# Routing tables of a two-stage expert kernel: one compare-and-scale instruction for each tile and choice on VectorE, in place of wide compares and a scaling pass on ScalarE

## The chip, the cores and the metric

The kernel runs on one core of a Trainium2 chip. The metric is the device time of one launch in microseconds (us). Of the kernel before there are three timed runs and one profiled execution. Numbers are float32; fp32r is the rounded form of it that the products of TensorE read.

## The reference, cut to what matters

4096 rows (8 sequences of 512) of 256 numbers pass four layers: an attention layer, a mixture of 8 experts with 2 chosen for each row, a recurrent mixing layer, and the same mixture of experts again. What matters here is what comes before each expert layer: the rows have to be sorted by expert.

```
scores = softmax(x @ gate_w.T);  top_scores, sel = top_k(scores, 2)
order = argsort(sel_flat, stable)       # rows grouped by expert
tok_sorted = order % N                  # which token stands at which sorted place
```

## The kernel before

The 4096 tokens are 32 tiles of 128 (one token for each partition), and each has two choices. The kernel has four phases: attention, experts, mix, experts. Attention and mix both end with the building of a table `row_token`: for each block of 128 sorted rows, the token of every row. The expert phase gathers its rows by that table, so it starts only when the table is there (all engines meet between two phases).

**How the table is made.** `posf` holds the sorted position of each token and choice; `positions` (L287) turns it to an integer and splits it into a lane (low 7 bits, `lane_at`) and a block (the rest, `block_at`). The tiles are taken in 8 groups of 4 (`CH` is 4). For group n:

- `hot_blocks` (L302), VectorE: a 0/1 table `block_hot`, 128 x (2 choices x 4 tiles x 120 blocks), that is 1 where the block number is the token's. One compare of 960 columns, line L308, with an integer operand that is spread along the columns and `lane`, a constant ramp.
- `hot_rows` (L313), VectorE: the same for the lane, 2 x 4 x 128 = 1024 columns, one compare, line L318, output fp32r.
- `send_tokens` (L322), ScalarE: four copies with a scale for each partition, L330, 240 columns each, that multiply `block_hot` by the token's number and write `sent` in fp32r.
- `place_tokens` (L395), TensorE: 8 products (choice x tile), L401, `sent` against `row_hot`, added up in one bank over all 8 groups.

After group 7, `region_rows` (ScalarE, L337) copies the bank, `final_places` (VectorE, L363, last instruction L377) makes `spot`, `order_tokens` (TensorE, L411) multiplies the two, and `row_tokens` (VectorE, L382 and L383) writes the table.

**Buffers.** `block_hot` is 2 deep in attention and 3 deep in mix; `sent` and `row_hot` are 3 deep in attention and 6 deep in mix. `hot_blocks` waits until ScalarE has used its buffer, `hot_rows` and `send_tokens` until TensorE has.

**The order around it, written out by hand.** The groups 0 to 5 ("early") cover tiles 0 to 23, whose choices are known one sequence before the end. In attention VectorE does, after its last period: `positions`, blocks(0), the statistics of the last sequence (L827, L830), rows(0), then blocks and rows of groups 1 to 5, then the top two experts of the last sequence (`softmax_begin`, first instruction MAX8 at L135), the late choices, `late_places` (which calls `positions` again), blocks and rows of groups 6 and 7, `final_places`, `row_tokens`. ScalarE puts its `send_tokens` between the steps of the last sequence's normalisation and gate. TensorE places group 0, then the gate transposes (L991), group 1, the gate products (L1002), groups 2 to 4, the count of the late choices, groups 5 to 7.

In mix, groups 0 to 3 stand inside VectorE's last period, ahead of `finish(b, 0)` (L1944), which joins the second half of a layer for GpSimd to add to x (L1786). Groups 4 and 5 follow, then the softmax of the sequence before the last (MAX8, L135), `finish(b, 1)`, the statistics of the last sequence, its softmax, and the late part as in attention. GpSimd turns the statistics into scales in four short instructions (L772 to L775 in attention, L1754 to L1759 in mix). An instruction that the next one reads is followed by a wait for it (`own.link`).

The three instructions of the step, shortened:

```
nc.vector.tensor_tensor(r.block_hot[n % depth], block_at..to_broadcast(shape), lane[:, 0:RB]..to_broadcast(shape), ALU.is_equal)
nc.vector.tensor_tensor(r.row_hot[n % depth], lane_at..to_broadcast(shape), lane..to_broadcast(shape), ALU.is_equal)
nc.scalar.activation(r.sent[..][:, :, j, :], r.block_hot[..][:, :, j, :], ACT.Copy, scale=const.token[:, t:t + 1])
```

Of the kernel before, what the change touches and what calls it, by code (L numbers as in the profile page):

```python
# [9 lines left out]
ALU = mybir.AluOpType  # L10
ACT = mybir.ActivationFunctionType
# [200 lines left out]
class Route:  # L212


    def __init__(self, hots, ranks, small, rounded, row_hot, block_hot, sent, bank, placed, sem):
# [9 lines left out]
        self.lane_at, self.block_at = s.take([P, TOPK, T], I32), s.take([P, TOPK, T], I32)  # L225
        self.counti = s.take([P, EX], I32)
# [4 lines left out]
        self.block_hot = [Shelf(f).take([P, TOPK, CH, RB]) for f in block_hot]  # L231
# [9 lines left out]
        self.block_hot_ready, self.row_hot_ready = sem("r_block_hot_ready"), sem("r_row_hot_ready")  # L241
        self.sent_ready, self.sent_used = sem("r_sent_ready"), sem("r_sent_used")
        self.region_ready, self.spot_ready, self.table_done = sem("r_region_ready"), sem("r_spot_ready"), sem("r_table_done")
# [57 lines left out]

def hot_blocks(nc, dve, r, const, n):  # L302

    depth = len(r.block_hot)
    if n >= depth:
        dve.wait_ge(r.sent_ready, n - depth + 1)
    shape = [P, TOPK, CH, RB]
    nc.vector.tensor_tensor(r.block_hot[n % depth], r.block_at[:, :, n * CH:(n + 1) * CH].unsqueeze(3).to_broadcast(shape),  # L308
                            const.lane[:, 0:RB].unsqueeze(1).unsqueeze(1).to_broadcast(shape),
                            ALU.is_equal).then_inc(r.block_hot_ready, 1)  # L310


def hot_rows(nc, dve, r, const, n):  # L313
    depth = len(r.row_hot)
    if n >= depth:
        dve.wait_ge(r.sent_used, n - depth + 1)
    shape = [P, TOPK, CH, P]
    nc.vector.tensor_tensor(r.row_hot[n % depth], r.lane_at[:, :, n * CH:(n + 1) * CH].unsqueeze(3).to_broadcast(shape),  # L318
                            const.lane[:].unsqueeze(1).unsqueeze(1).to_broadcast(shape), ALU.is_equal).then_inc(r.row_hot_ready, 1)


def send_tokens(nc, act, r, const, n):  # L322

    depth = len(r.sent)
    act.wait_ge(r.block_hot_ready, n + 1)
    if n >= depth:
        act.wait_ge(r.sent_used, n - depth + 1)
    for j in range(CH):
        t = n * CH + j
        last = nc.scalar.activation(r.sent[n % depth][:, :, j, :], r.block_hot[n % len(r.block_hot)][:, :, j, :], ACT.Copy,  # L330
                                    scale=const.token[:, t:t + 1])
    last.then_inc(r.sent_ready, 1)

# [168 lines left out]
def phase_attention(nc, x_dram, qk_w, qk_b, lepe_w, lepe_b, gate_s, cos_t, sin_t,  # L502
# [10 lines left out]
    with ExitStack() as ctx:  # L513
# [3 lines left out]
        def sem(name):  # L517
# [66 lines left out]
        route = Route(lepe_flat[:], xn_flat[0][:], qk_flat[:], xnT_flat[2][:], [hi_flat[:], lo_flat[:], xnT_flat[0][:]],  # L584
                      [ex_flat[:, 0:2 * N], ex_flat[:, 2 * N:4 * N]], [lepe_hi_flat[:], lepe_lo_flat[:], xnT_flat[3][:]],
                      (l1, q1, q0), placed, lambda name: sem("a_" + name))
# [76 lines left out]
        def _(act):  # L663
# [85 lines left out]

            over_batches(act, period)  # L750
            send_tokens(nc, act, route, const, 0)
            route_before(B)
            send_tokens(nc, act, route, const, 1)
            gate_rows(B)
            send_tokens(nc, act, route, const, 2)
            send_tokens(nc, act, route, const, 3)
            gate_logits(B)
            send_tokens(nc, act, route, const, 4)
            row_exp(B)
            send_tokens(nc, act, route, const, 5)  # L760
            row_finish(B)
            for n in range(EARLY, GROUPS):
                send_tokens(nc, act, route, const, n)
            region_rows(nc, act, route)
# [56 lines left out]
        def _(dve):  # L821
# [141 lines left out]
            positions(nc, placing, route, slice(0, TE))  # L963
            hot_blocks(nc, dve, route, const, 0)
# [12 lines left out]
            for n in range(EARLY, GROUPS):  # L977
                hot_blocks(nc, dve, route, const, n)
                hot_rows(nc, dve, route, const, n)
# [439 lines left out]
def phase_mix(nc, vec, w_key, w_value, w_recept, w_output, f_w_key, f_w_recept, f_w_value, gate_s,  # L1419
# [7 lines left out]
    with ExitStack() as ctx:  # L1427
# [3 lines left out]
        def sem(name):  # L1431
# [49 lines left out]
        route = Route(flat["xnT"], flat["eps"], flat["al"], over[12][:], [o[:] for o in over[0:6]],  # L1481
                      [flat["be"], xn[:].rearrange("p t c -> p (t c)"), flat["dT"]], [o[:] for o in over[6:12]],
                      (xb_[5], xb_[5], xb_[0]), placed, sem)
# [4 lines left out]
        def static(b, value):  # L1488
            return isinstance(b, int) and b == value
# [60 lines left out]
        def _(act):  # L1550
# [146 lines left out]
            def period(b):  # L1697
# [27 lines left out]
                if has_next(b, 1):  # L1725
                    carry(b + 1)
                if static(b, B - 1):
                    send_tokens(nc, act, route, const, 0)
# [4 lines left out]
            for n in range(1, 4):  # L1733
                send_tokens(nc, act, route, const, n)
            gate_logits(B - 2)
            row_exp(B - 2)
            row_finish(B - 2)
            for n in range(4, EARLY):
                send_tokens(nc, act, route, const, n)
            route_norm(B - 1)  # L1740
# [3 lines left out]
            row_finish(B - 1)  # L1744
            for n in range(EARLY, GROUPS):
                send_tokens(nc, act, route, const, n)
            region_rows(nc, act, route)
# [64 lines left out]
        def _(dve):  # L1812
# [157 lines left out]
            def period(b):  # L1970
# [27 lines left out]
                if static(b, B - 1):  # L1998
                    early_ranks(nc, dve, placing, route, const)
                    early_bases(nc, placing, route, const)  # L2000
                    early_places(nc, placing, route)
                    positions(nc, placing, route, slice(0, TE))
                    early_homes(nc, placing, route, const)
                    for n in range(4):
                        hot_blocks(nc, dve, route, const, n)
                        hot_rows(nc, dve, route, const, n)
# [3 lines left out]
            for n in range(4, EARLY):  # L2010
                hot_blocks(nc, dve, route, const, n)
                hot_rows(nc, dve, route, const, n)
# [9 lines left out]
            for n in range(EARLY, GROUPS):  # L2022
                hot_blocks(nc, dve, route, const, n)
                hot_rows(nc, dve, route, const, n)
# [266 lines left out]
```

## Time and profile before

| what | value |
|---|---|
| timed runs | 1454.54 us median of 3 (1452.37 to 1456.57) |
| the profiled execution's own time | 1455.75 us |
| its span, first to last instruction | 1454.0 us |
| mean granted clock of TensorE | 0.959 of full speed |
| busy in the span: TensorE products, VectorE, ScalarE, GpSimd | 1330.3, 918.4, 674.5, 621.1 us |

The profiled execution took 1.2 us more than the median run. A row of the timeline reads: start in us, duration in us (of several merged, from the first's start to the last's end), engine, line, operation, output<-input, partitions x columns and type, count, and in brackets the idle time before it and what ended it. DVE is VectorE, ACT is ScalarE, POOL is GpSimd, PE is TensorE. On VectorE the next instruction's row can start before the last one's has ended; the distance from start to start is what an instruction takes of the engine's time.

### The profile page before, as it was taken

The numbers are of one execution on the slowest core, as the hardware profiler recorded it, in microseconds if no ns is written. First come the engines' busy times: TensorE is split into PE (matmuls) and PEld (weight loads), VectorE is DVE, ScalarE is ACT, GpSimd is POOL, SyncE is SP. The second block draws the span as 40 slices with busy tenths as digits, with TensorE's granted clock in tenths as the row PEclk, the third lists the DMA queues.
The fourth block names the chain that finished last, engine by engine and source line by source line (L and its number), as shares of the span: only waits on it lengthen the run. The fifth ranks groups of instructions, "written<-read, shape, count | busy, mean of one in ns | idle before, by whom it ended". The sixth has DMA issues, their size and how long they took to land. (4 is left out here: it accounts for less than half of the span.)

```text
span 1454.0 us, 27881 instructions
## 1 busy us (share of the span) xinstructions
PE 1330.3 (91%) x7610; PEld 1130.9 (78%) x7611; DVE 918.4 (63%) x2176; ACT 674.5 (46%) x1508; POOL 621.1 (43%) x563
## 2 busy tenths in 40 slices
PE   4899996799999999926899999998969999999996
PEld 4899995688888888823677787777857888888885
DVE  4777888554444444438889999987854444454543
ACT  3476764333333333324766678666642333333332
POOL 3667762255555555421223223222214555555553
PEclk9899997799999999968999999999979999999999
DMA  6376765466665333260000000000326666643332
GB/s 225 145 272 207 269 215 199 155 159 166 159 163 119 59 51 57 46 220 0 1 15 1 30 29 29 29 0 30 117 76 180 163 162 161 165 72 53 52 58 33
DMA packets 100873, 157.84 MB, mean 109 GB/s; under 512 B 10256, under 2 KB 60688, under 8 KB 100816
## 3 DMA queue, kind: packets, MB, share of 16 engines
q1 hardware_dynamic: 73120, 118.67, 24.0%
q0 software_dynamic: 27264, 37.82, 16.2%
q10 hardware_dynamic: 432, 0.66, 0.2%
q8 instruction: 28, 0.46, 0.1%
q14 instruction: 29, 0.24, 0.1%
HBM read 95.89 MB, written 61.21 MB: 108 GB/s over the span
## 5 line engine op out<-in xcount | busy, mean ns | idle before, releaser
L1214 POOL DMA_INDIRECT out_x<-second_y,second_add_token x71 | 112.5, 1585 | 154.3 <-ACT second_y L1246 85.0
L1214 POOL DMA_INDIRECT x_rows<-first_y,first_add_token x71 | 112.5, 1585 | 154.2 <-ACT first_y L1246 84.6
L1317 DVE TENSOR_TENSOR first_hT_lo<-bank,first_hT_hi 128x512 fp32r<-128x512 f32 x71 | 49.1, 692 | 161.1 <-ACT first_hT_hi L1238 161.1
L1317 DVE TENSOR_TENSOR second_hT_lo<-bank,second_hT_hi 128x512 fp32r<-128x512 f32 x71 | 49.1, 692 | 160.0 <-ACT second_hT_hi L1238 160.0
L163 PE MATMUL bank<-ring,first_xT_hi 128*128 x284 | 118.4, 417 | 2.2 <-DVE first_xT_lo L1305 2.2
L163 PE MATMUL bank<-ring,second_xT_hi 128*128 x284 | 118.4, 417 | 2.1 <-DVE second_xT_lo L1305 2.1
L164 PE MATMUL bank<-ring,first_xT_hi 128*128 x284 | 112.6, 396 | 0.0
L164 PE MATMUL bank<-ring,second_xT_hi 128*128 x284 | 112.6, 396 | 0.0
L165 PE MATMUL bank<-ring,second_xT_lo 128*128 x284 | 112.4, 396 | 0.0
L165 PE MATMUL bank<-ring,first_xT_lo 128*128 x284 | 112.0, 394 | 0.0
L2041 PE MATMUL bank<-b_fv,b_hT 128*128 128x256 f32 x480 | 106.8, 381 | 0.0
L2041 PEld LDWEIGHTS bank<-b_fv,b_hT 128*128 128x128 f32 x480 | 91.2, 191 | 12.1
L1245 ACT ACTIVATE first_add_token<-row_token 128x1 uint32 (+1 forms) x71 | 14.4, 203 | 177.6 <-DMA x_rows<-first_y,first_add_token 118.7
L1245 ACT ACTIVATE second_add_token<-row_token 128x1 uint32 (+1 forms) x71 | 14.4, 203 | 177.6 <-DMA out_x<-second_y,second_add_token 113.6
L1786 POOL TENSOR_TENSOR x<-x,b_fs 128x512 f32<-128x512 f32 (+1 forms) x16 | 25.3, 1583 | 146.1 <-DVE b_fs L1944 146.1
L1205 POOL DMA_INDIRECT second_xs<-normed_rows,second_gather_token x71 | 71.1, 1002 | 23.2 <-issue 21.6
L1205 POOL DMA_INDIRECT first_xs<-normed_rows,first_gather_token x71 | 71.2, 1002 | 23.0 <-issue 21.7
L1381 PE MATMUL bank<-ring,first_hT_hi 128*128 x284 | 76.7, 303 | 0.8 <-ACT first_hT_hi L1238 0.8
L1381 PE MATMUL bank<-ring,second_hT_hi 128*128 x284 | 76.5, 302 | 0.8 <-ACT second_hT_hi L1238 0.8
L1264 ACT ACTIVATE second_g<-bank 128x512 f32<-128x512 f32 x71 | 42.4, 598 | 64.1 <-PE bank L165 64.1
L1264 ACT ACTIVATE first_g<-bank 128x512 f32<-128x512 f32 x71 | 42.4, 598 | 63.4 <-PE bank L165 63.4
L1382 PE MATMUL bank<-ring,first_hT_hi 128*128 x284 | 70.6, 281 | 0.0
(412 smaller groups left out, 3960.5 us busy)
## 6 DMA issues: line engine op xcount, KB each, us to landing
ring<-split_weights SPq DMA_DIRECT2D x192, 256.0 KB, 3.2
a_wraw<-in_L_ffn_w SPq DMA_DIRECT2D x24, 512.0 KB, 6.8
split_weights<-a_whi SPq DMA_DIRECT2D x24, 512.0 KB, 2.7
split_weights<-a_wlo SPq DMA_DIRECT2D x24, 512.0 KB, 3.6
normed_rows<-xg SPq DMA_DIRECT2D x16, 528.0 KB, 3.7
x_rows<-x SPq DMA_DIRECT2D x8, 512.0 KB, 7.6
x<-x_rows SPq DMA_DIRECT2D x8, 512.0 KB, 6.7
out_x<-x SPq DMA_DIRECT2D x8, 512.0 KB, 2.8
```

Source lines behind the costliest of these rows:

```text
L163: nc.tensor.matmul(out, hi, other_hi, start=start, stop=False)
L164: nc.tensor.matmul(out, hi, other_lo, start=False, stop=False)
L165: return nc.tensor.matmul(out, lo, other_hi, start=False, stop=stop)
L1205: nc.gpsimd.indirect_dma_start(xs[q][:], None, normed_dram[:], bass.IndirectOffsetOnAxis(ap=gather_token[q][:], axis=0)).then_inc(loaded[q ...
L1214: nc.gpsimd.indirect_dma_start(x_dram[:], bass.IndirectOffsetOnAxis(ap=add_token[q][:], axis=0), y[q], None, compute_op=ALU.add).then_inc( ...
L1245: nc.scalar.activation(add_token[q][:], column(row_token, i), ACT.Copy)
L1264: nc.scalar.activation(g[par][:], a_bank[par][:], ACT.Silu).then_inc(silu_done, 1)
L1317: nc.vector.tensor_tensor(hT_lo[par][:].rearrange("p k t -> p (k t)"), th_bank[par][:], hT_hi[par][:].rearrange("p k t -> p (k t)").bitcas ...
L1381: nc.tensor.matmul(y_bank[:, 0:C], hT_hi[par][:, k, :], w_hi[:, k * C:(k + 1) * C], start=(k == 0), stop=False)
L1382: nc.tensor.matmul(y_bank[:, 0:C], hT_hi[par][:, k, :], w_lo[:, k * C:(k + 1) * C], start=False, stop=False)
L1786: nc.gpsimd.tensor_tensor(xt, xt, fs[:, h, :].rearrange("p (t c) -> p t c", c=C), ALU.add).then_inc(x3_ready, 1)
L2041: last = nc.tensor.matmul(out[:, j * C:(j + 1) * C], src(i, j), w[:, i, :], start=(i == 0), stop=(i == chunks - 1))
```

## The change

`hot_blocks` and ScalarE's `send_tokens` are gone, with the buffers and the semaphore between them. A new `send_tokens` on VectorE writes `sent` directly: for each choice and tile one TENSOR_SCALAR of 120 columns that compares the constant ramp with the token's block (a value for each partition) and multiplies by the token's number (another). `hot_rows` becomes 8 TENSOR_SCALARs of 128 columns with one value for each partition. Both need the block and the lane as float32, so `positions` gets two more copies. `send_tokens` now waits for TensorE's use of `sent`, as `hot_rows` does. The places in VectorE's order are those of `hot_blocks` before.

```diff
@@ positions
     own.link(nc.vector.tensor_scalar(r.block_at[:, :, tiles], r.posi[:, :, tiles], 7, None, ALU.arith_shift_right))
+    nc.vector.tensor_copy(r.lanef[:, :, tiles], r.lane_at[:, :, tiles])
+    own.link(nc.vector.tensor_copy(r.blockf[:, :, tiles], r.block_at[:, :, tiles]))
@@
-def hot_blocks(nc, dve, r, const, n):
-    depth = len(r.block_hot)
-    if n >= depth:
-        dve.wait_ge(r.sent_ready, n - depth + 1)
-    nc.vector.tensor_tensor(r.block_hot[n % depth], ..., ALU.is_equal).then_inc(r.block_hot_ready, 1)
+def send_tokens(nc, dve, r, const, n):
+    depth = len(r.sent)
+    if n >= depth:
+        dve.wait_ge(r.sent_used, n - depth + 1)
+    for k in range(TOPK):
+        for j in range(CH):
+            t = n * CH + j
+            last = nc.vector.tensor_scalar(r.sent[n % depth][:, k, j, :], const.lane[:, 0:RB], r.blockf[:, k, t:t + 1],
+                                           const.token[:, t:t + 1], ALU.is_equal, ALU.mult)
+    last.then_inc(r.sent_ready, 1)
@@ hot_rows
-    nc.vector.tensor_tensor(r.row_hot[n % depth], ..., ALU.is_equal).then_inc(r.row_hot_ready, 1)
+    for k in range(TOPK):
+        for j in range(CH):
+            t = n * CH + j
+            last = nc.vector.tensor_scalar(r.row_hot[n % depth][:, k, j, :], const.lane[:], r.lanef[:, k, t:t + 1], None, ALU.is_equal)
+    last.then_inc(r.row_hot_ready, 1)
@@
-def send_tokens(nc, act, r, const, n):
-    act.wait_ge(r.block_hot_ready, n + 1)
-    if n >= depth:
-        act.wait_ge(r.sent_used, n - depth + 1)
-    for j in range(CH):
-        last = nc.scalar.activation(..., ACT.Copy, scale=const.token[:, t:t + 1])
-    last.then_inc(r.sent_ready, 1)
@@ ScalarE, both phases: every send_tokens(nc, act, route, const, n) removed
@@ VectorE, both phases: every
-                hot_blocks(nc, dve, route, const, n)
+                send_tokens(nc, dve, route, const, n)
```

## Rows read from the trace of the kernel before

**Rows 1.** The page, busy time, share of the span and instructions of each engine.

```profile
PE 1330.3 (91%) x7610; PEld 1130.9 (78%) x7611; DVE 918.4 (63%) x2176; ACT 674.5 (46%) x1508; POOL 621.1 (43%) x563
```

**Rows 2.** Windows: stretch, length, busy PE, PEld, DVE, ACT, POOL, clock, DMA share, GB/s.

```profile
280.00:1000.00 720.00, 673.26 (x3503) 547.59 (x3502) 485.79 (x981) 359.14 (x741) 268.15 (x250) 0.97 0.30 71
...
231.66:250.84 19.18, 13.74 (x74) 11.98 (x75) 15.08 (x20) 10.94 (x27) 5.26 (x4) 0.68 0.60 198
...
1038.32:1055.42 17.10, 17.10 (x93) 15.33 (x92) 15.10 (x14) 12.37 (x29) 2.02 (x1) 1.00 0.25 91
...
1071.41:1083.76 12.35, 4.31 (x19) 3.85 (x19) 9.69 (x38) 6.01 (x23) 0.00 (x0) 0.50 0.13 44
```

**Rows 3.** Timeline of DVE, end of attention, early groups.

```profile
231.66 1.16 DVE L308 TENSOR_TENSOR a_ex<-a_qk_raw,lane 128x960 f32<-128x960 int32 x1
...
234.59 1.19 DVE L318 TENSOR_TENSOR a_qk_hi<-a_qk_raw,lane 128x1024 fp32r<-128x1024 int32 x1
...
243.93 1.16 DVE L308 TENSOR_TENSOR a_ex<-a_qk_raw,lane 128x960 f32<-128x960 int32 x1 [3.74 <-ACT a_lepe_lo L330]
...
250.84 0.37 DVE L135 MAX8 a_tp<-a_lg 128x8 f32<-128x8 f32 x4
```

**Rows 4.** Timeline of DVE and POOL, end of mix, early groups.

```profile
1038.32 1.16 DVE L308 TENSOR_TENSOR b_be<-b_al,lane 128x960 f32<-128x960 int32 x1
...
1049.32 0.69 DVE L1944 SCALAR_TENSOR_TENSOR b_fs<-b_fs,bank 128x512 f32<-128x512 f32 x1 [1.43 <-PE bank L2097]
...
1050.19 2.02 POOL L1786 TENSOR_TENSOR x<-x,b_fs 128x512 f32<-128x512 f32 x1 [14.93 <-DVE b_fs L1944]
...
1051.00 2.30 DVE L318 TENSOR_TENSOR b_over<-b_al,lane 128x1024 fp32r<-128x1024 int32 x1
...
1055.42 0.36 DVE L135 MAX8 b_tp<-b_lg 128x8 f32<-128x8 f32 x4
```

**Rows 5.** Timeline of all engines, end of mix, late groups 6 and 7.

```profile
1076.16 0.17 DVE L290 TENSOR_SCALAR b_al<-b_al 128x16 int32<-128x16 int32 x1
1076.36 1.16 DVE L308 TENSOR_TENSOR b_be<-b_al,lane 128x960 f32<-128x960 int32 x1
...
1078.57 1.15 DVE L308 TENSOR_TENSOR b_xn<-b_al,lane 128x960 f32<-128x960 int32 x1
...
1080.78 0.17 DVE L367 TENSOR_TENSOR b_al<-b_al 128x8 f32<-128x8 f32 x1
...
1081.56 1.83 PE L401 MATMUL bank<-b_over 128*120 128x128 f32 x8 [0.37 <-ACT b_over L330]
...
1082.61 0.32 DVE L377 TENSOR_SCALAR b_over<-blocks,b_al,lane_of 128x72 fp32r<-128x72 f32 x1
1083.43 0.28 ACT L337 ACTIVATE b_over<-bank 120x128 fp32r<-120x128 f32 x1 [2.02 <-PE bank L401]
...
1083.76 0.43 PE L411 MATMUL bank<-b_over 120*128 120x72 f32 x1 [0.36 <-ACT b_over L337]
```

**Rows 6.** Timeline of DVE in three other places: instructions with and without per-partition values.

```profile
16.13 0.42 DVE L862 TENSOR_SCALAR a_nsin<-a_sin 128x512 f32<-128x512 f32 x1
...
63.07 0.36 DVE L912 TENSOR_SCALAR a_kz<-head_mask,a_ksum 128x8 f32<-128x8 f32 x2
63.34 0.68 DVE L913 TENSOR_TENSOR a_kB<-bank,a_nsin 128x512 f32<-128x512 f32 x1
63.94 0.68 DVE L914 TENSOR_TENSOR a_kB<-bank,a_sin 128x512 f32<-128x512 f32 x1
...
660.37 1.41 DVE L1879 SCALAR_TENSOR_TENSOR b_rho<-b_k,vectors,b_eps 128x512 f32<-128x512 f32 x2
661.70 1.22 DVE L1833 TENSOR_TENSOR b_dT<-b_xnT 128x1024 f32<-128x1024 f32 x1
```

**Rows 7.** By line and shape, ACT: one buffer's share of the scaling copies.

```profile
L330 ACT ACTIVATE a_lepe_hi<-a_ex,token 128x240 fp32r<-128x240 f32 x12 | 4.9, 483 | 6.3 <-DVE a_ex L308 6.3
```

**Rows 8.** Timeline of ACT, end of attention: the last sequence's logits.

```profile
247.85 0.17 ACT L684 ACTIVATE a_lg<-bank 128x32 f32<-128x32 f32 x1
```

More of the change, by code:

```diff
@@ L212, with __init__ @@
 class Route:
-    def __init__(self, hots, ranks, small, rounded, row_hot, block_hot, sent, bank, placed, sem):
+    def __init__(self, hots, ranks, small, rounded, row_hot, sent, bank, placed, sem):
         self.hot = Shelf(hots).take([P, TOPK, EX, T])
@@ L225, in __init__ @@
         self.lane_at, self.block_at = s.take([P, TOPK, T], I32), s.take([P, TOPK, T], I32)
+        self.lanef, self.blockf = s.take([P, TOPK, T]), s.take([P, TOPK, T])
         self.counti = s.take([P, EX], I32)
@@ L230, in __init__ @@
         self.row_hot = [Shelf(f).take([P, TOPK, CH, P]) for f in row_hot]
-        self.block_hot = [Shelf(f).take([P, TOPK, CH, RB]) for f in block_hot]
         self.sent = [Shelf(f).take([P, TOPK, CH, RB]) for f in sent]
@@ L240, in __init__ @@
         self.counts_read = sem("r_counts_read")
-        self.block_hot_ready, self.row_hot_ready = sem("r_block_hot_ready"), sem("r_row_hot_ready")
+        self.row_hot_ready = sem("r_row_hot_ready")
         self.sent_ready, self.sent_used = sem("r_sent_ready"), sem("r_sent_used")
@@ L316, in hot_rows @@
         dve.wait_ge(r.sent_used, n - depth + 1)
-    shape = [P, TOPK, CH, P]
-    nc.vector.tensor_tensor(r.row_hot[n % depth], r.lane_at[:, :, n * CH:(n + 1) * CH].unsqueeze(3).to_broadcast(shape),
-                            const.lane[:].unsqueeze(1).unsqueeze(1).to_broadcast(shape), ALU.is_equal).then_inc(r.row_hot_ready, 1)
-def send_tokens(nc, act, r, const, n):
-    depth = len(r.sent)
-    act.wait_ge(r.block_hot_ready, n + 1)
-    if n >= depth:
-        act.wait_ge(r.sent_used, n - depth + 1)
-    for j in range(CH):
-        t = n * CH + j
-        last = nc.scalar.activation(r.sent[n % depth][:, :, j, :], r.block_hot[n % len(r.block_hot)][:, :, j, :], ACT.Copy,
-                                    scale=const.token[:, t:t + 1])
-    last.then_inc(r.sent_ready, 1)
+    for k in range(TOPK):
[3 more added lines that the diff above has]
+    last.then_inc(r.row_hot_ready, 1)
 def region_rows(nc, act, r):
@@ L584, in phase_attention @@
         route = Route(lepe_flat[:], xn_flat[0][:], qk_flat[:], xnT_flat[2][:], [hi_flat[:], lo_flat[:], xnT_flat[0][:]],
-                      [ex_flat[:, 0:2 * N], ex_flat[:, 2 * N:4 * N]], [lepe_hi_flat[:], lepe_lo_flat[:], xnT_flat[3][:]],
+                      [lepe_hi_flat[:], lepe_lo_flat[:], xnT_flat[3][:]],
                       (l1, q1, q0), placed, lambda name: sem("a_" + name))
@@ L750, in _ @@
             over_batches(act, period)
-            send_tokens(nc, act, route, const, 0)
             route_before(B)
-            send_tokens(nc, act, route, const, 1)
             gate_rows(B)
-            send_tokens(nc, act, route, const, 2)
-            send_tokens(nc, act, route, const, 3)
             gate_logits(B)
-            send_tokens(nc, act, route, const, 4)
             row_exp(B)
-            send_tokens(nc, act, route, const, 5)
             row_finish(B)
-            for n in range(EARLY, GROUPS):
-                send_tokens(nc, act, route, const, n)
             region_rows(nc, act, route)
@@ L963, in _ @@
             positions(nc, placing, route, slice(0, TE))
-            hot_blocks(nc, dve, route, const, 0)
+            send_tokens(nc, dve, route, const, 0)
             dve.wait_ge(x1_ready, 2 * B)
@@ L977, in _ @@
             for n in range(EARLY, GROUPS):
-                hot_blocks(nc, dve, route, const, n)
+                send_tokens(nc, dve, route, const, n)
                 hot_rows(nc, dve, route, const, n)
@@ L1481, in phase_mix @@
         route = Route(flat["xnT"], flat["eps"], flat["al"], over[12][:], [o[:] for o in over[0:6]],
-                      [flat["be"], xn[:].rearrange("p t c -> p (t c)"), flat["dT"]], [o[:] for o in over[6:12]],
+                      [o[:] for o in over[6:12]],
                       (xb_[5], xb_[5], xb_[0]), placed, sem)
@@ L1726, in period @@
                     carry(b + 1)
-                if static(b, B - 1):
-                    send_tokens(nc, act, route, const, 0)
                 if has_before(b, 1):
@@ L1732, in _ @@
             over_periods(act, period)
-            for n in range(1, 4):
-                send_tokens(nc, act, route, const, n)
             gate_logits(B - 2)
@@ L1737, in _ @@
             row_finish(B - 2)
-            for n in range(4, EARLY):
-                send_tokens(nc, act, route, const, n)
             route_norm(B - 1)
@@ L1744, in _ @@
             row_finish(B - 1)
-            for n in range(EARLY, GROUPS):
-                send_tokens(nc, act, route, const, n)
             region_rows(nc, act, route)
@@ L2004, in period @@
                     for n in range(4):
-                        hot_blocks(nc, dve, route, const, n)
+                        send_tokens(nc, dve, route, const, n)
                         hot_rows(nc, dve, route, const, n)
@@ L2010, in _ @@
             for n in range(4, EARLY):
-                hot_blocks(nc, dve, route, const, n)
+                send_tokens(nc, dve, route, const, n)
                 hot_rows(nc, dve, route, const, n)
@@ L2022, in _ @@
             for n in range(EARLY, GROUPS):
-                hot_blocks(nc, dve, route, const, n)
+                send_tokens(nc, dve, route, const, n)
                 hot_rows(nc, dve, route, const, n)
```

4 lines of the change are left out of this document (removed).

## The prediction

> **What bounds the kernel now.** The page comes first: TensorE is busy for 91% of the span, VectorE for 63% [rows 1], so the bulk of the run is TensorE's, and there the share of time is what it looks like: from 280 to 1000 us TensorE works 673 of 720 us [rows 2]. The change touches only two short stretches ahead of the expert phases, so the second view is the windows of these. At the end of attention (231.66 to 250.84 us) VectorE is busy 15.1 of 19.2 us and TensorE 13.7, partly with products that only keep it busy; in the last 12.35 us of mix VectorE is busy 9.7, ScalarE 6.0, TensorE 4.3, and its clock is 0.50 of full, the 1.2 GHz level [rows 2]. There the order of VectorE sets the time. The third view, the timeline, says how: in attention VectorE has one idle stretch of 3.74 us, for a buffer that ScalarE's scaling holds, and goes from its last early compare straight to MAX8 [rows 3]; in mix it waits 1.43 us for TensorE ahead of L1944, and then goes through groups 4 and 5 to MAX8 without a pause [rows 4]. In the late part the chain is: VectorE's compares, ScalarE's scaling of group 7, TensorE's products (L401), the copy L337, the product L411 [rows 5]. Nothing else can run beside these two stretches: the expert phase waits for the table.
>
> **The price of the new instructions.** The removed work: a group's two compares take 2.21 us of VectorE, from 1076.36 to 1078.57 and again to 1080.78 [rows 5]: 1.08 for 960 columns, 1.13 for 1024. ScalarE's four copies take 0.48 each [rows 7].
>
> The added ones are priced by start-to-start distances. (a) A short instruction: four MAX8 of 8 columns span 0.36 to 0.37 us [rows 3, 4]; with about 0.155 for the last alone that leaves 0.07 for each, of which 8 columns are 0.01. So the fixed part is some 0.065 us. (b) A value for each partition: two L912 (8 columns, one such value) take 63.34 - 63.07 = 0.27, 0.135 each, 0.065 more than the short instruction. The same surcharge shows at 512 columns: L913 without one takes 63.94 - 63.34 = 0.60, L1879 with one takes (661.70 - 660.37)/2 = 0.665 [rows 6]. (c) Columns: L913 gives 0.60 - 0.065 for 512, 1.04 ns each. A TENSOR_SCALAR goes at twice that: L862 takes 0.42 for 512 columns, where L913 takes 0.68 [rows 6]. (d) Two values, a compare and an fp32r output at once: only L377 has it, 72 columns in 0.32 us [rows 5]. One L912 lasts 0.225 (0.36 - 0.135); plus a second surcharge 0.065 and 64 more columns at half price 0.033 gives 0.32. At full price it would be 0.35. So L377 speaks for both: the second value costs again, and the compare into fp32r runs at two columns a cycle.
>
> Hence one `send_tokens` instruction is 0.065 + 2 x 0.065 + 120 x 0.52 ns = 0.257 us, one of `hot_rows` 0.065 + 0.065 + 0.067 = 0.197 us. A group: 8 x 0.257 + 8 x 0.197 = 2.05 + 1.57 = 3.62 us, in place of 2.21: **+1.41 us of VectorE for a group**. For the distance of two-value instructions no row exists, only L377's duration; the low bound is a second value that hides behind the first (0.193), the high one is that with full-price columns (0.319).
>
> The Trainium skill (page "VectorE: DVE Perf Modes", section on the TRN2 errata) prices an instruction between SBUF tensors as 58 cycles plus the columns over the mode's speed-up, with no term for a per-partition value. By that both kinds would take about 0.12 to 0.13 us and a group about 2.0; L912 with its 0.135 at 8 columns, where that formula gives 0.065, speaks against it, and the result of it is one of the rivals. The same section also says that many small tiles pay the fixed part each time.
>
> **Part by part.**
>
> *The two copies in `positions`.* The first adds about 0.1 us, the second, with a wait behind it, 0.2, as L290 does (1076.16 to 1076.36) [rows 5]. +0.3 at each of four places.
>
> *End of attention, early.* From the first compare to MAX8 is 19.18 us, with the statistics between (234.59 - 231.66 - 1.08 = 1.85) and the idle 3.74 [rows 3]. After: 0.3 + 2.05 + 1.85 + 1.57 + 5 x 3.62 = 23.87 us. **+4.7.** The idle time goes: its cause, ScalarE's copies behind the normalisation, is no more, and `sent` waits for TensorE three groups back. By TensorE's order group 1 stands behind the normalisation and its transposes. Now ScalarE is through its first copies behind the normalisation 12.3 us after the first table (243.93), and the statistics will come 1.3 us later; group 4, the first that wants group 1's buffer, comes after 0.3 + 2.05 + 1.85 + 1.57 + 3 x 3.62 = 16.6 us. So I count no wait. The logits come no later than now (ScalarE has no copies in their way), and VectorE arrives at MAX8 after them, so their gain is worth nothing.
>
> *End of mix, early.* Groups 0 to 3 start at 1038.62 and take 14.48: L1944 starts at 1053.10, not 1049.32 [rows 4]. What covers 1.43 us now (the wait for TensorE) is used up. L1944 takes 0.61, groups 4 and 5 take 7.24: MAX8 at 1060.95. Then GpSimd: while L1786 ran (1050.19 to 1052.21), L318 lasted 2.30 in place of 1.22, a loss of 1.08 [rows 4]. The new instructions are short, so GpSimd gets in at once, and a little more than that should be lost: I take 1.2, between nothing and the whole 2.02 of L1786. MAX8 at 1062.15 in place of 1055.42: **+6.7.** Behind MAX8 wait the softmax of the sequence before the last, `finish(b, 1)`, GpSimd's addition, the last statistics and the whole gate: all of it is shifted, since VectorE is the last to come. TensorE, done with its values earlier, only waits longer.
>
> *Late part, in both phases.* Now L401 of group 7 starts 5.20 us after the first compare [rows 5], held by ScalarE's copies. After: 0.3 + 4 halves of groups 6 and 7, 7.24, + 0.15 for the last instruction to end and release = 7.69. **+2.5** in each phase. ScalarE's 1.65 us behind the last block table leave the chain; that gain is in this difference. `final_places` starts 3.1 us later and takes the 2.15 it takes now (1080.78 to 1082.93); the table bank's copy L337 is then ready some 0.2 us after it, so L411 moves by the same 2.5. Group 6's products (1.83 us at the low clock) end ahead of group 7's tables.
>
> *ScalarE.* 64 copies go, 31 us of busy time, almost all beside other work: worth nothing beyond what is counted. No DMA moves.
>
> **Sum.** 4.7 + 2.5 + 6.7 + 2.5 = +16.4 us on the profiled execution: 1455.75 + 16.4 = 1472.1. The median lies 1.2 lower: **1471 us**. Not known within it: how long GpSimd's four short instructions in attention (5.26 us busy there [rows 2]) hold VectorE: from nothing to the 2 us of L1786 in mix [rows 4], taken as nothing, since L318 beside them ran at 1.19 [rows 3]; and in mix 0 to 2 in place of 1.2. Own range 1467 to 1475.
>
> **Rivals.**
>
> *One column a cycle.* If the compare into fp32r doesn't get the doubled rate, an instruction costs 0.062 to 0.067 more, a group 1.03, and all 16 groups lie on the path: +16.5, **1487 us**. Against it: L377 fits 0.32 and not 0.35 [rows 5]. 8%.
>
> *The second value is free* in a stream of such instructions: 8 x 0.064 = 0.51 less for a group, 8.2 in all, **1463 us**. L377's duration speaks against it, but a duration isn't a distance. 6%.
>
> *The per-partition values are read ahead, beside the instruction before.* Then the place that decides is the early part of attention: a group costs 8 x (0.128 + 0.131) = 2.07 us, just under the 2.21 of now, so the 3.74 us of idle time are won and nothing is paid. Groups would bring MAX8 to 0.3 + 1.03 + 1.85 + 1.05 + 5 x 2.07 = 14.6 us after the first table, but the logits are there at 248.02 only, now behind ScalarE's copies [rows 8]; without these I take 0.7 us earlier, 3.5 before MAX8's time now; the late parts gain 0.6 each (0.3 + 4.14 + 0.15 = 4.6 against 5.2) and the early part of mix 0.2 where GpSimd holds it. Sum -4.9: **1449.6 us**, faster. It turns at a group price of about 2.3 us. For it: the idle time is there and ScalarE's step is on the late chain. Against it: L912 and L1879 both show the surcharge in the distance, not only in the duration [rows 6]. 6%.
>
> *Something between these two* within 4.4 us of now: 2%.
>
> **Chances.** The forecast has 78%. 0.3% (4.4 us) is about what a measurement of this kernel can tell from no change. Faster by more 5%, within 3%, slower by more 92%. The range has to hold 8 in 10: own range, down to the free second value, and up a little for GpSimd's contention: 1462 to 1478; the one-column case stays outside.
>
> **What would show it.** In the changed profile: about 64 + 64 TENSOR_SCALARs of 120 and 128 columns in all at each phase's end, with durations near 0.34 and 0.28 us and distances of 0.257 and 0.197; a group every 3.6 us; no idle time in attention's early part; MAX8 in attention some 24 us after the first table's place now; L401 of group 7 released by VectorE, not ScalarE; 7.7 us from the first late table to it. The forecast is wrong if the distance of the two-value form is under 0.2 or over 0.3, if MAX8 in either phase waits for the logits, or if VectorE stands idle for TensorE's release of `sent`.

## The result, and the profile after the change

The changed kernel takes 1472.85 us (median of 4 runs, 1470.92 to 1474.62) where the kernel before, run beside it, takes 1455.55 us: a ratio of 1.0121, 95% interval 1.0108 to 1.0135. It is slower by 17.6 us (0.0121 x 1455.55). The forecast was 1471 us, its range 1462 to 1478. The profiled execution has a span of 1471.9 us, 17.9 more than the 1454.0 of before.

First the page of the changed kernel (busy time, share, instructions), which answers to [rows 1]:

```profile
PE 1332.4 (91%) x7610; PEld 1132.5 (77%) x7611; DVE 941.1 (64%) x2408; ACT 650.0 (44%) x1444; POOL 616.5 (42%) x563
```

VectorE has 232 more instructions and only 22.7 us more busy time, ScalarE 64 fewer and 24.5 us less. That says nothing yet of where 17.9 us come from: TensorE's share hasn't moved. So the run is cut at marks that both kernels have. These rows of before, from the timelines of VectorE and TensorE, are such marks beside those in [rows 3 to 5]: the first copy of `positions` (L288), the MAX8 that follows, the order product (L411); L308, L908 and L193 are for further down.

```profile
61.87 1.28 DVE L908 SCALAR_TENSOR_TENSOR a_el<-a_ex,bank 128x512 f32<-128x512 f32 x2 [0.20 <-DVE bank L901]
...
230.05 0.19 DVE L288 CAST a_qk_raw<-a_qk_raw 128x48 int32<-128x48 f32 x1
...
246.43 1.16 DVE L308 TENSOR_TENSOR a_ex<-a_qk_raw,lane 128x960 f32<-128x960 int32 x1 [0.21 <-ACT a_xnT L330]
...
263.20 0.43 PE L411 MATMUL bank<-a_xnT 120*128 120x72 f32 x1 [0.37 <-ACT a_xnT L337]
...
1037.22 0.19 DVE L288 CAST b_al<-b_al 128x48 int32<-128x48 f32 x1
...
1045.60 1.16 DVE L308 TENSOR_TENSOR b_be<-b_al,lane 128x960 f32<-128x960 int32 x1 [0.57 <-ACT b_over L330]
...
1063.41 2.96 PE L193 MATMUL bank<-b_fk_hi 128*128 128x512 f32 x12
...
1071.41 0.37 DVE L135 MAX8 b_tp<-b_lg 128x8 f32<-128x8 f32 x4 [8.98 <-ACT b_lg L1668]
```

**Attention.** VectorE, GpSimd and TensorE in the changed kernel's timeline; `send_tokens` is L313, `hot_rows` L325, the order product now L405:

```profile
230.73 0.18 DVE L288 CAST a_qk_raw<-a_qk_raw 128x48 int32<-128x48 f32 x1
232.65 2.11 DVE L313 TENSOR_SCALAR a_lepe_hi<-lane,a_qk_raw,token 128x120 fp32r<-128x120 f32 x8
...
236.52 1.65 DVE L325 TENSOR_SCALAR a_qk_hi<-lane,a_qk_raw 128x128 fp32r<-128x128 f32 x8
...
237.88 1.17 POOL L760 TENSOR_TENSOR a_mv<-a_mv,neg_half 128x4 f32<-128x4 f32 x1
238.10 2.10 DVE L313 TENSOR_SCALAR a_lepe_lo<-lane,a_qk_raw,token 128x120 fp32r<-128x120 f32 x8
240.11 1.65 DVE L325 TENSOR_SCALAR a_qk_lo<-lane,a_qk_raw 128x128 fp32r<-128x128 f32 x8
...
256.02 0.36 DVE L135 MAX8 a_tp<-a_lg 128x8 f32<-128x8 f32 x4
...
270.82 0.43 PE L405 MATMUL bank<-a_xnT 120*128 120x72 f32 x1 [0.37 <-ACT a_xnT L331]
```

To be read here: between the first table and MAX8 VectorE waits for no other engine any more, where it waited 3.74 us before [rows 3] and 0.21 us at 246.43. Eight instructions of 120 columns take 240.11 - 238.10 = 2.01 us from start to start, 0.252 each, eight of 128 columns 238.10 - 236.52 = 1.58 (1.57 elsewhere), 0.196 each. A group costs 3.59 us in place of 2.21. The row's duration (2.11, 1.65) is the wrong price: it holds the last instruction's end, which overlaps the next one's start.

**Mix, up to the gate.** The same engines:

```profile
1045.31 0.19 DVE L288 CAST b_al<-b_al 128x48 int32<-128x48 f32 x1
1046.73 2.11 DVE L313 TENSOR_SCALAR b_over<-lane,b_al,token 128x120 fp32r<-128x120 f32 x8
...
1061.08 0.68 DVE L1922 SCALAR_TENSOR_TENSOR b_fs<-b_fs,bank 128x512 f32<-128x512 f32 x1
1061.68 3.06 DVE L313 TENSOR_SCALAR b_over<-lane,b_al,token 128x120 fp32r<-128x120 f32 x8
1061.94 1.46 POOL L1764 TENSOR_TENSOR x<-x,b_fs 128x512 f32<-128x512 f32 x1 [18.59 <-DVE b_fs L1922]
...
1069.81 0.36 DVE L135 MAX8 b_tp<-b_lg 128x8 f32<-128x8 f32 x4
...
1076.95 5.46 PE L193 MATMUL bank<-b_fk_hi 128*128 128x512 f32 x12 [5.95 <-DVE b_mvg L1800]
...
1087.03 0.37 DVE L135 MAX8 b_tp<-b_lg 128x8 f32<-128x8 f32 x4 [10.22 <-ACT b_lg L1654]
```

L1922 (L1944 before) has lost its wait for TensorE, as forecast: VectorE comes later than TensorE's values. The group behind it takes 3.06 us in place of 2.11, since GpSimd's addition runs beside it: 0.95 lost. Then something that the forecast doesn't have: TensorE idles 5.95 us behind MAX8, and the same 12 products that keep it busy, 2.96 us before, take 5.46.

**Late part of mix**, all engines, which answers to [rows 5]:

```profile
1091.78 0.17 DVE L290 TENSOR_SCALAR b_al<-b_al 128x16 int32<-128x16 int32 x1
1092.27 2.11 DVE L313 TENSOR_SCALAR b_over<-lane,b_al,token 128x120 fp32r<-128x120 f32 x8
1094.30 1.65 DVE L325 TENSOR_SCALAR b_over<-lane,b_al 128x128 fp32r<-128x128 f32 x8
...
1099.60 1.86 PE L395 MATMUL bank<-b_over 128*120 128x128 f32 x8 [1.73 <-DVE b_over L325]
...
1101.82 0.43 PE L405 MATMUL bank<-b_over 120*128 120x72 f32 x1 [0.37 <-ACT b_over L331]
```

The products of group 7 (L395) are now released by VectorE's last compare, not by ScalarE, and start 7.33 us after the first L313, where they started 5.20 after the first compare.

The windows between the same marks (stretch, length, busy PE, PEld, DVE, ACT, POOL, clock, DMA share, GB/s), against [rows 2]:

```profile
232.65:256.02 23.37, 13.41 (x76) 11.93 (x76) 23.21 (x104) 3.36 (x7) 2.40 (x4) 0.65 0.47 160
...
1046.73:1069.81 23.08, 23.08 (x140) 21.04 (x139) 23.08 (x97) 6.03 (x12) 1.46 (x1) 1.00 0.15 57
1069.81:1087.03 17.22, 10.64 (x52) 8.65 (x50) 3.58 (x24) 5.79 (x21) 2.97 (x5) 0.70 0.18 62
1087.03:1101.82 14.79, 4.13 (x18) 3.64 (x18) 12.71 (x68) 2.71 (x15) 0.00 (x0) 0.59 0.11 37
```

and of the kernel before, the stretch of the gate that [rows 2] lack:

```profile
1055.42:1071.41 15.99, 14.44 (x100) 12.58 (x98) 3.57 (x24) 8.88 (x29) 2.97 (x5) 1.00 0.19 67
```

VectorE is busy all through both early stretches. In the gate's window its work is the same (3.57 and 3.58), yet the window is 1.23 us longer, at a granted clock of 0.70 in place of 1.00. In shorter windows of the changed kernel the clock is 1.00 until 1071, where TensorE's products end, 0.50 from 1073 to 1082, and 1.00 again from 1083.

Five stretches between such marks hold 16.9 of the 17.9 us. The table has them for all ten kernels, in us, each a difference of two timeline rows, taken before rounding, so that the last digit can differ by one from the rows shown. Early goes from the copy L288 to MAX8 (in mix the first of two), gate from mix's first MAX8 to its last, late from the last MAX8 to the order product.

| kernel | attention early | attention late | mix early | mix gate | mix late | sum |
|---|---|---|---|---|---|---|
| before | 20.80 | 12.36 | 18.20 | 15.99 | 12.35 | 79.70 |
| changed | 25.29 | 14.80 | 24.50 | 17.21 | 14.80 | 96.60 |
| e1 rows only | 21.91 | 13.00 | 18.98 | 16.00 | 12.98 | 82.87 |
| e2 send only | 22.71 | 13.84 | 21.88 | 16.93 | 13.85 | 89.21 |
| e3 extra value | 28.16 | 15.76 | 27.41 | 16.60 | 15.75 | 103.68 |
| e4 idle copies | 25.29 | 14.79 | 24.56 | 17.27 | 14.78 | 96.69 |
| e5 keep warm | 25.36 | 14.81 | 24.57 | 15.99 | 14.79 | 95.52 |
| e6 sends ahead | 17.72 | 12.82 | 18.19 | 15.99 | 12.35 | 77.07 |
| e7 ahead and warm | 17.77 | 13.21 | 18.17 | 16.00 | 11.69 | 76.84 |
| e8 count first | 17.62 | 12.37 | 18.16 | 15.99 | 11.68 | 75.82 |

The change costs 4.49 + 2.44 + 6.30 + 1.22 + 2.45 = 16.9 us in the five. The other 1.0 of the span lies outside; the part from attention's order product to mix's first copy was 774.0 us before, 774.5 after, and between 773.4 and 776.5 in the experiments, so 1 us there isn't assigned to anything.

### The profile page after: what moved, and what is told of

The parts are those of the page before. It is cut to its first block and busy times, and to the rows that moved or that the text cites. A ratio compares the mean times of both kernels' runs of the same rounds, so it can differ in the third digit from the quotient of the medians.

```text
span 1471.9 us, 28042 instructions
## 1 busy us (share of the span) xinstructions
PE 1332.4 (91%) x7610; PEld 1132.5 (77%) x7611; DVE 941.1 (64%) x2408; ACT 650.0 (44%) x1444; POOL 616.5 (42%) x563
## 5 line engine op out<-in xcount | busy, mean ns | idle before, releaser
L1367 PE MATMUL bank<-ring,second_hT_hi 128*128 x284 | 76.6, 302 | 0.8 <-ACT second_hT_hi L1224 0.8
L1368 PE MATMUL bank<-ring,second_hT_hi 128*128 x284 | 70.6, 281 | 0.0
```

Of the source, the lines that this page charges most:

```text
L1367: nc.tensor.matmul(y_bank[:, 0:C], hT_hi[par][:, k, :], w_hi[:, k * C:(k + 1) * C], start=(k == 0), stop=False)
L1368: nc.tensor.matmul(y_bank[:, 0:C], hT_hi[par][:, k, :], w_lo[:, k * C:(k + 1) * C], start=False, stop=False)
```

## The experiments

The theory: the short instructions cost what their distances say, VectorE is the only engine that counts in the four early and late stretches, and the gate's 1.2 us come from TensorE's clock. The rivals: the second value costs nothing, ScalarE's copies were worth something, the gate's loss has to do with VectorE or GpSimd.

**e1: only `hot_rows` changed.**

```diff
 kernel before, with
+    own.link(nc.vector.tensor_copy(r.lanef[:, :, tiles], r.lane_at[:, :, tiles]))
-    nc.vector.tensor_tensor(r.row_hot[n % depth], ..., ALU.is_equal)      # 1024 columns
+    8 x nc.vector.tensor_scalar(..., const.lane[:], r.lanef[:, k, t:t + 1], None, ALU.is_equal)
```

> The kernel before with only the row tables changed: hot_rows becomes 8 one-value TENSOR_SCALARs, blocks and ScalarE's scaling stay as they were. My theory (VectorE's own time on the path, 1.57 against 1.13 us for a group's rows): late part +0.6 in each phase, attention's early part +1 to +1.5 because the idle 3.7 us hides groups 0 to 2, mix's early part +1 to +1.5 because the 1.4 us wait for TensorE hides groups 0 to 3; +3 to +4.5 us in all. Rival (the time comes from the block tables alone, not from the rows): within 1 us of before. Rival (each group costs the path its whole surcharge everywhere): 16 x 0.44 + 0.8 = +7.8.

Measured: ratio 1.0038 (1.0024 to 1.0053), five stretches +3.2 us. From the timeline of VectorE in attention:

```profile
239.82 1.16 DVE L310 TENSOR_TENSOR a_ex<-a_qk_raw,lane 128x960 f32<-128x960 int32 x1 [0.78 <-ACT a_lepe_lo L334]
...
243.91 1.16 DVE L310 TENSOR_TENSOR a_ex<-a_qk_raw,lane 128x960 f32<-128x960 int32 x1 [1.37 <-ACT a_xnT L334]
```

Six groups at 0.44 more are 2.64 us, and the copy with its own wait adds 0.30 (1.91 us from L288's place to the first compare in place of 1.61): 2.94 us of work. VectorE's waits were 3.74 and 0.21; 0.78 + 1.37 = 2.15 are left, so 1.80 us have been filled. 2.94 - 1.80 = 1.14, and attention's early part grew by 1.11. In mix the work is 2.64 + 0.22, and VectorE had 1.43 us of idle time ahead of L1944 [rows 4] and 0.57 at 1045.60, for ScalarE's scaling (the row of L308 above); no row of e1 carries either wait. 2.86 - 2.00 = 0.86, and mix's early part grew by 0.78. So idle time of VectorE does cover added work, until it is used up.

**e2: only `send_tokens` changed.**

```diff
 changed kernel, with
-    8 x nc.vector.tensor_scalar(..., r.lanef[:, k, t:t + 1], None, ALU.is_equal)
+    nc.vector.tensor_tensor(r.row_hot[n % depth], ..., ALU.is_equal)      # 1024 columns
-    nc.vector.tensor_copy(r.lanef[:, :, tiles], r.lane_at[:, :, tiles])
```

> The changed kernel with the wide compare of before for the rows; only the block tables are made and scaled by two-value TENSOR_SCALARs. My theory: a group takes 2.05 + 1.13 = 3.18 us of VectorE in place of 2.21; attention early +2, attention late +1.5, mix early +4, mix late +1.5: +8 to +10 us against before. Rival (taking ScalarE's scaling out of the chain pays for the block tables, and the loss is the rows'): within 2 us of before.

Measured: ratio 1.006 (1.0038 to 1.0082), five stretches +9.5 us. VectorE late in mix:

```profile
1086.30 2.10 DVE L312 TENSOR_SCALAR b_over<-lane,b_al,token 128x120 fp32r<-128x120 f32 x8
1088.32 1.22 DVE L322 TENSOR_TENSOR b_over<-b_al,lane 128x1024 fp32r<-128x1024 int32 x1
1089.45 0.16 DVE L358 TENSOR_TENSOR b_al<-b_al 128x8 f32<-128x8 f32 x1
```

Side by side in one kernel: eight short instructions 2.02 us, one wide 1.13. The two halves add up to 3.2 + 9.5 = 12.7, the whole costs 16.9. Of the missing 4.2, 3.3 lie in the early parts. They are mostly the idle times, which each half could use for itself and the two together only once: in attention's early part 1.11 + 1.91 = 3.0 against 4.49, in mix's 0.78 + 3.68 = 4.5 against 6.30.

**e3: one more value in `hot_rows`**, a multiplication by 1.0, which stands in a table as a value for each partition.

```diff
-    r.lanef[:, k, t:t + 1], None, ALU.is_equal)
+    r.lanef[:, k, t:t + 1], const.keep_early[:, 1:2], ALU.is_equal, ALU.mult)
```

> The changed kernel with one more per-partition value (1.0) in each hot_rows instruction; output and everything else unchanged. My theory (every per-partition value costs 0.064 us of the engine's time, in the distance from start to start too, and all 16 groups lie on the path): distance of the row instructions 0.197 to 0.261, 16 x 8 x 0.064 = +8.2 us above the changed kernel, +25 above before. Rival (a second value hides behind the first): no difference to the changed kernel, and then the two-value instructions' 0.251 has another cause.

Measured: ratio 1.016 (1.0133 to 1.0186), five stretches 103.68 against 96.60. VectorE late in mix:

```profile
1099.71 2.11 DVE L313 TENSOR_SCALAR b_over<-lane,b_al,token 128x120 fp32r<-128x120 f32 x8
1101.73 2.14 DVE L325 TENSOR_SCALAR b_over<-lane,b_al,keep_early 128x128 fp32r<-128x128 f32 x8
1103.78 2.10 DVE L313 TENSOR_SCALAR b_over<-lane,b_al,token 128x120 fp32r<-128x120 f32 x8
```

1103.78 - 1101.73 = 2.05 us for eight, where the same eight with one value take 1.57: 0.060 us for each second value, in the distance, in a stream of nothing else. The rival of the free second value falls with this row. Each of the four stretches grew as VectorE's work did (six groups by 0.48 are 2.88; attention early 2.87, mix early 2.91; two groups are 0.96; late 0.96 and 0.95). Together that is 7.69 us; the gate gave 0.61 back, so the five grew by 7.08, less than the 8.2 expected.

The edit adds a second operation along with the second value, so the operation could be what costs. The trace of before speaks against it: L908 does two operations on 512 columns, with a constant 1.0 written into the instruction and no value for each partition, and its two instructions take (63.07 - 61.87)/2 = 0.60 us each [rows 6], as L913 does with one operation. L1879, with two operations and one such value, takes 0.665. The same shows for TENSOR_SCALAR in the changed kernel, on one partition and with two operations and two constants (`min` with 7, `add` of 1):

```profile
276.29 0.19 DVE L1274 TENSOR_SCALAR first_ready_at<-first_past 1x72 int32<-1x72 f32 x1
276.41 0.18 DVE L1275 TENSOR_SCALAR first_slot_at<-first_expert_at 1x72 int32<-1x72 int32 x1
```

It takes 0.12 us for 72 columns, where L289, with one operation and one constant, takes 0.10 for 48 (230.27 to 230.37 before); two values would make it an estimated 0.23. By these rows it is the value read for each partition that costs, not the operation.

**e4: ScalarE's copies back, for nobody.** The 32 scaling copies of each phase at their old places, between spare buffers; nobody waits for them.

```diff
 changed kernel, with
+def scale_idle(nc, act, idle, const, n):
+    4 x nc.scalar.activation(idle[1][:, 240 columns], idle[0][:, 240 columns], ACT.Copy, scale=const.token[:, t:t + 1])
 and scale_idle(..., n) wherever ScalarE had send_tokens(..., n)
```

> The changed kernel with ScalarE's 64 scaling copies put back where they stood, on spare buffers that nothing waits for. My theory (the copies were worth nothing except through the chain to TensorE, which is gone): late parts unchanged, attention's early part unchanged since VectorE comes last there, +0 to +0.5 us against the changed kernel. Rival (relieving ScalarE is worth something by itself and has kept the loss small): +2 us or more.

Measured: ratio 1.0104 (1.0073 to 1.0135), an interval that holds the changed kernel's 1.0121. ScalarE and VectorE in attention:

```profile
244.95 3.33 ACT L336 ACTIVATE a_ex<-a_ex,token 128x240 f32<-128x240 f32 x8
248.18 0.17 ACT L690 ACTIVATE a_lg<-bank 128x32 f32<-128x32 f32 x1
...
255.26 0.36 DVE L135 MAX8 a_tp<-a_lg 128x8 f32<-128x8 f32 x4
```

The logits' copy comes at 248.18, right behind eight copies of 3.33 us; MAX8 comes 7.1 us later and doesn't wait for it. All five stretches are those of the changed kernel within 0.06. What the change took from ScalarE was worth nothing by itself.

**e5: TensorE kept busy where it idled.** Twenty more filler products behind the early tables of mix, ahead of its wait for the last statistics.

```diff
                 place_tokens(nc, pe, route, n)
+            keep_busy(nc, xb_[1][:], fk_hi[:, 0, 0:P], fk_hi[:, 0, 0:N], 20)
             pe.wait_ge(fs_ready, 2 * B)
```

> The changed kernel with 20 products more that only keep TensorE busy, in mix, behind the early placements and ahead of the wait for the last statistics. The stretch from the first MAX8 to the last one in mix took 15.99 us before and 17.21 in the changed kernel, without a table in it. My theory (VectorE's delay leaves TensorE idle for 6 us, it falls to the lower clock, and the 12 warming products then take 5.5 us and hold the gate transposes): the stretch goes back to 16.0 to 16.2, -1.1 us. Rival (the 1.2 us are waits between VectorE, ScalarE and GpSimd): the stretch stays at 17.2.

TensorE in mix:

```profile
1068.42 4.79 PE L193 MATMUL bank<-b_fk_hi 128*128 128x512 f32 x20
...
1074.55 2.96 PE L193 MATMUL bank<-b_fk_hi 128*128 128x512 f32 x12 [1.35 <-DVE b_mvg L1800]
```

The 20 fill the idle time down to 1.35 us, the 12 of the gate are back at 2.96, and the gate's stretch is 15.99, to 0.01 that of before, with VectorE's and GpSimd's work untouched. The granted clock of the gate's stretch is 1.00 again, where it was 0.70. So the 1.22 us are the clock's, which fell while TensorE idled. The time of the whole run doesn't resolve so small a gain: ratio 1.0119 (1.0104 to 1.0134) against 1.0121, though the profiled span is 1468.2 against 1471.9. That is more than the gain explains: 2.5 us of it lie ahead of the first stretch (L288 in attention at 228.21 in place of 230.73).

**e6: the idle time won with the wide compares.** The change used up VectorE's 3.74 us of idle time in attention and paid too much for it. Here it is used up with `before`'s instructions: `block_hot` gets four buffers instead of two (on `kB` and `qA`, free by then), ScalarE scales a group ahead of the normalisation, TensorE places one more group ahead of the logits.

```diff
-                      [ex_flat[:, 0:2 * N], ex_flat[:, 2 * N:4 * N]],
+                      [ex_flat[:, 0:2 * N], ex_flat[:, 2 * N:4 * N], kB (flat), qA (flat)],
 ScalarE, attention
             send_tokens(nc, act, route, const, 0)
-            route_before(B)
             send_tokens(nc, act, route, const, 1)
-            gate_rows(B)
+            route_before(B)
             send_tokens(nc, act, route, const, 2)
+            gate_rows(B)
             send_tokens(nc, act, route, const, 3)
 TensorE, attention
             place_tokens(nc, pe, route, 1)
+            place_tokens(nc, pe, route, 2)
             gate_products(B)
```

> The kernel before, the idle 3.7 us of VectorE in attention taken away another way: block_hot 4 deep (two dead buffers), ScalarE's scaling of group 1 ahead of the last normalisation and of group 2 ahead of the gate rows, TensorE's placing of group 2 ahead of the gate products. My theory (the idle time was ScalarE's order and the two buffers): early part of attention 20.8 to about 17.8 us, all else the same, -2.5 to -3 us, ratio 0.998. Rival (the logits or TensorE's release of the row tables then hold VectorE just as long): less than 1 us.

Measured: ratio 0.9983 (0.9974 to 0.9992), faster than before by 2.5 us. VectorE and TensorE in attention:

```profile
242.81 1.22 DVE L318 TENSOR_TENSOR a_qk_lo<-a_qk_raw,lane 128x1024 fp32r<-128x1024 int32 x1 [0.88 <-PE bank L401]
...
246.15 0.37 DVE L135 MAX8 a_tp<-a_lg 128x8 f32<-128x8 f32 x4
...
247.25 1.83 PE L401 MATMUL bank<-a_qk_lo,a_lepe_lo 128*120 128x128 f32 x8 [1.02 <-ACT a_lepe_lo L330]
248.88 0.36 PE L391 MATMUL bank<-a_xnT,before 128*128 128x64 f32 x1
```

VectorE waits only 0.88 us now, and MAX8 comes 17.72 us after the first copy instead of 20.80. But the late part grew by 0.46: the count of the choices (L391), which the late positions need, stands behind a group's products in TensorE's order, 1.83 us at the low clock. That this is the cause is shown by e8.

**e7: the same with more filler products**, ahead of the count and of groups 5 to 7 in attention, and ahead of the count and of groups 6 and 7 in mix.

```diff
 attention
+            keep_busy(nc, q2[:], ..., 3)
             count_choices(nc, pe, route, const, 1)
+            keep_busy(nc, q2[:], ..., 4), (6), (3) ahead of place_tokens of groups 5, 6, 7
 mix
+            keep_busy(nc, xb_[1][:], ..., 5)
             count_choices(nc, pe, route, const, 1)
+            keep_busy(nc, xb_[1][:], ..., 13), (3) ahead of place_tokens of groups 6, 7
```

> e6_sends_ahead with products that only keep TensorE busy put between the late placements of both phases, where its clock stood at 1.2 GHz. My theory (a group's 8 products take 1.83 us at that level and 1.03 at the other, and those of the last group lie on the path): late parts 12.35 to 11.6 us each, -1.5 us beyond e6. Rival (the added products delay the count or the placements, or the clock does not rise in time): late parts the same or up to 1 us longer.

Measured: ratio 0.9989 (0.9978 to 1.0), no better than e6. TensorE in attention and in mix:

```profile
247.21 1.59 PE L193 MATMUL bank<-a_xnT 128*128 128x512 f32 x3
248.60 0.26 PE L391 MATMUL bank<-a_xnT,before 128*128 128x64 f32 x1
...
1071.11 5.25 PE L193 MATMUL bank<-b_fk_hi 128*128 128x512 f32 x13
...
1078.68 1.03 PE L401 MATMUL bank<-b_over 128*120 128x128 f32 x8 [0.43 <-ACT b_over L330]
```

It went both ways. In mix, where fillers run in time that is idle anyway, the last group's products took 1.03 us instead of 1.83 and the late part became 0.66 us shorter. In attention they were themselves slow (3 in 1.59 us, at a granted clock of 0.50) and stood ahead of the count: late part 13.21 where e6 has 12.82.

**e8: e6 with the count put first in attention, and e7's fillers in mix alone.**

```diff
 TensorE, attention, kernel e6 with
-            for n in range(3, EARLY - 1):
-                place_tokens(nc, pe, route, n)
+            place_tokens(nc, pe, route, 3)
             count_choices(nc, pe, route, const, 1)
-            for n in range(EARLY - 1, GROUPS):
+            for n in range(4, GROUPS):
                 place_tokens(nc, pe, route, n)
```

> e6_sends_ahead with TensorE's count of the late choices ahead of its placing of group 4 in attention, and with the warming products of e7_ahead_and_warm in mix alone. My theory: attention's early part stays at 17.7 us; its late part, 12.82 in e6 because the count waited 0.35 us for group 4's products at the low clock, goes back to 12.4; mix's late part 11.7 as in e7; in all -3.8 us against before, ratio 0.9975 or less. Rival (the 0.46 us came from ScalarE's later copies): attention's late part stays at 12.8.

Measured: 1450.95 us, median of 11 runs, beside 1454.73 for the kernel before; ratio 0.997 (0.9959 to 0.9982). TensorE in attention and in mix:

```profile
249.84 0.42 PE L391 MATMUL bank<-a_xnT,before 128*128 128x64 f32 x1 [2.14 <-DVE a_xnT L345]
...
1077.68 1.03 PE L401 MATMUL bank<-b_over 128*120 128x128 f32 x8 [0.43 <-ACT b_over L330]
```

The count now waits for VectorE alone, and attention's late part is back at 12.37 with the early part's gain kept. The five stretches are 75.82 us, 3.9 under before, and the medians differ by 3.8. This version beats both kernels; it has the wide compares.

## Why the prediction was right

The forecast's mechanism held in the four stretches where VectorE makes tables, and its sum was close: 16.4 us of terms against 16.9 in the five stretches. Part of the closeness is luck: four terms were a little too high, and a fifth, the gate's, was missing. The forecast also counts from a median of 1454.54 us, and the kernel before, run beside the changed one, took 1455.55; against that the change cost 17.3 to 17.6 us. Point by point:

- **The price of an instruction.** Put at 0.257 and 0.197 us, it is 0.252 and 0.196; a group 3.59, not 3.62. e3 measured the part for which the trace of before had no distance, 0.060 for a second value, put at 0.065. The rival of one column a cycle wanted 0.06 more for each instruction, and isn't there. The rival of values read ahead wanted 0.13.
- The formula of the Trainium skill (page "VectorE: DVE Perf Modes", section on the TRN2 errata), fixed part plus columns over the speed-up, gives an estimated 0.12 to 0.13 for either. The rows disagree by the values' price, 0.06 for each one. What the same section of the Trainium skill says of many small tiles paying the fixed part each time, they bear out: eight instructions of 128 columns take 1.57 us, one of 1024 takes 1.13.
- **`positions`.** +0.3 forecast, +0.31 and +0.32 at the two early places (230.73 to 232.65 against 230.05 to 231.66, and 1.42 against 1.10), 0.29 late (L290 to the first table, 0.49 in place of 0.20).
- **Attention early.** +4.7 forecast, +4.49 found. The six groups at 0.03 less each make up 0.18 of the difference. The statistics took 1.85 between (236.52 - 232.65 - 2.02), as before; no wait for `sent` or for the logits came, and GpSimd's short instructions held nothing up (2.01 and 1.58 beside them).
- **Mix early.** +6.7 forecast, +6.30 found. 23.08 us from the first L313 are 6 x 3.59 + 0.60 + 0.95, to 0.01. Of the 0.43 too much, GpSimd's hold is 0.25 (taken as 1.2, found 0.95) and the groups are 0.18.
- **Late parts.** +2.5 forecast, +2.44 and +2.45 found. The 7.69 us to group 7's products hold the 0.3 of `positions`: found are 0.29 + 7.33 = 7.62. The change of releaser came as forecast.
- **The gate: the step that failed.** The prediction says that everything behind MAX8 is shifted, and that TensorE "only waits longer". It did wait, and its clock fell for it: +1.22 us that the sum doesn't have. The clue was in the rows: [rows 2] show the late stretch at 0.50 where TensorE has little to do, and the gate's products stand on the path. The four terms that were too high, by 0.7 us in all, hid half of this.
- **ScalarE.** Worth nothing in itself: e4 shows it. Its step did leave the late chain, but only together with VectorE's longer work: in e2, which takes the same step out, the late parts are still 1.5 us longer. The prediction puts the 64 copies at 31 us of busy time, by their durations; the page has 24.5 less. The idle times that they made on VectorE, 3.74 and 0.21 us in attention and 0.57 in mix, are used up by the new instructions. The 0.21 and the 0.57 the prediction didn't see; since it built the new stretches up from their instructions, its times don't hang on them.

One cause isn't separated: how much of the 1.0 us outside the five stretches belongs to the change. The same part of the run scatters by 3 us from profile to profile.

## What to carry to other kernels

Price a row of small instructions by start-to-start distances, with a term for each per-partition value: here an estimated 0.065 us fixed and 0.06 for each value outweighed the halved column time, and one wide compare of 1024 columns (1.13 us) beats eight of 128 (1.57) although each of its columns costs about twice as much (an estimated 1.04 ns against 0.52). Where an engine's idle time is the prize, look first at whose buffer or place in the order makes it: two more buffers and a changed order won 3 us that the new instructions overpaid. And when a stretch is made longer, follow every engine that now idles up to its next work on the path: TensorE's came back slower.

## What the runs showed of the hardware

- **A pause of TensorE costs twice.** After 5.95 us in which it waited, 12 products of 512 columns took 5.46 us (granted clock of the window 0.70), where they took 2.96 without a pause (before) and after one of 1.35 (e5). The loss isn't a constant: the changed kernel's gate lost 1.22 us by it; e3's, after a pause of 5.94 and with the 12 products in 5.10, lost 0.61. There the clock was back ahead of the gate's transposes (8 products in 1.03 us, where the changed kernel's took 1.31); why it rose sooner stays open. In e7 fillers helped where they ran in idle time (mix: late part 12.35 to 11.69), and cost where they stood ahead of work that was due (attention: 12.82 to 13.21).
- **GpSimd ran faster beside short instructions of VectorE.** Its four small operations in attention were busy 5.26 us beside compares of 1.1 us [rows 2] and 2.40 beside instructions of 0.2 us; the addition in mix took 1.46 in place of 2.02 [rows 4], and cost VectorE 0.95 us, where it had cost 1.08. With VectorE idle it takes 1.26 (at 1073.58 in the changed kernel), and four small operations like the others take 1.70 (mix, from 1077.00). What holds the two engines up, no run here shows.
- **A value of 1.0 costs like any other.** The second value for each partition took 0.060 us in each instruction although it changes nothing in the output. A constant written into the instruction, 1.0 too, cost nothing that shows (L908).
